# Joining the two halves of the routing sums on VectorE before one turning, instead of turning both and joining after

## The chip, the cores and the metric

The kernel runs on one core of one Trainium2 chip. The metric is device microseconds (us) of one execution; lower is better. Engines: TensorE (PE, with its weight loads shown apart as PEld), VectorE (DVE), ScalarE (ACT), GpSimd (POOL), and SyncE (SP), which issues all DMAs of this kernel.

## The reference, cut to what matters

```python
def reference(x, cond, weights, router_weight, router_bias, expert_bias):
    W = weights[cond]                                    # (64, 128, 128), one of 16 per batch
    h = jnp.einsum('bct,bcd->bdt', x, W)                 # x: (64, 128, 2048) f32
    flat = h.reshape(64 * 128, 2048)
    logits = jnp.einsum('th,eh->te', flat, router_weight) + router_bias    # 64 experts
    scores = jax.nn.softmax(logits, axis=-1)
    topk_w, topk_idx = jax.lax.top_k(scores, 8)
    w_sum = topk_w.sum(axis=-1, keepdims=True)
    w_dense = zeros.at[rows, topk_idx].add(topk_w)       # (8192, 64)
    out = flat * w_sum + w_dense @ expert_bias
    return x + out.reshape(64, 128, 2048)
```

The kernel gets the logits without h: it first forms z = x @ router_weight^T for a batch (128 channels by 64 experts) and then multiplies by the batch's W.

## The kernel before, in words

The 64 batches are taken in 32 pairs. A pair passes through three steps: in its *new* step its x is transposed and multiplied by the router, in its *mid* step the routing is finished (logits, top 8, exponentials, weights), in its *old* step the large product is formed and stored. So one step of the loop works on three pairs at once: new pair i, mid pair i-1, old pair i-2. Each engine has its own program, written out in a fixed order; a step has eight slots, v = 0 to 7, and semaphores tie the engines together. Four steps are unrolled in a loop body.

Products that need more than one pass's precision are made from two parts: a rounded part ("hi") and what is left ("lo"), both in fp32r. The router table router_hl holds hi and lo parts of the 64 experts side by side as 128 columns, so the router product has 128 rows: rows 0 to 63 are the sums with the high part, rows 64 to 127 those with the low part. zt_ps (one PSUM bank) holds that product for both batches of the pair, batch 0 in columns 0 to 127 and batch 1 in columns 128 to 255. High and low rows must still be added, and the sum turned (channels to partitions).

Per step and engine, in the order of the slots:

- TensorE: `transposes` (L325, four 128x128 transposes into a bank of xt_ps; none in slots 2 and 3, where VectorE re-lays the data), `project` (L385, L386, L387, L390, L391: five 512-column matmuls into a bank of p_ps), in slot 0 the last `route` of the mid pair (L337), in slots 2, 4 and 6 a `route` of the new pair (eight 256-column matmuls each), `turn_z` in slot 1 (L351, two transposes of zt_sb into scores_ps, with a wait for zt_ready), `score` in slot 3 (L360), `turn_kept` in slot 7 (L369). In slot 0 of the next step, project's fourth matmul (L390) waits for kept_t_ready.
- ScalarE: `zt_copy` in slot 1 (L470, the whole of zt_ps to zt_sb, 128x256), `xt_high` in each slot (L451), `x_high` (L459), `w_high` in slot 3 (L465), `exponentials` in slot 4 (L478, L482), `norm` in slot 6 (L499, L503), `kept_high` in slot 7 (L490).
- VectorE: `xt_low` in each slot (L546), `finish` in each slot (L612), `relay` at the end of slots 0 and 1 (L556), `z_sum` in slot 2 (L563, adds the two halves of the turned sums into z_sb), `add_bias` in slot 3 (L570), `top` in slot 4 (L577 to L583), `keep` in slot 5 (L591, L595), `kept_low` in slot 7 (L599). Within a slot the order is xt_low, top, kept_low, z_sum, keep, finish, add_bias, relay.
- GpSimd: `x_low` (L681) and `w_low` (L671). SyncE: loads and stores in one fixed order.

A pair's mid step is thus a chain over the engines: last route, zt_copy, turn_z, z_sum, score, add_bias, top, exponentials, keep, norm, turn_kept, kept_high, kept_low, and at its end the L390 of the next step.

Of the kernel before, what the change touches and what calls it, by code (L numbers as in the profile page):

```python
# [36 lines left out]
ALU = mybir.AluOpType  # L37
ACT = mybir.ActivationFunctionType
AX = mybir.AxisListType

P = 128
# [9 lines left out]
def adaln_router(nc, x, condition, weights, router_weight, router_bias, expert_bias, out):  # L51
    B, C, T = x.shape
    S, _, D = weights.shape
    E = router_weight.shape[0]
# [12 lines left out]
    with ExitStack() as ctx:  # L67
        def sb(name, shape, dt=F32):
            return ctx.enter_context(nc.sbuf_tensor(name, shape, dt))

        def bank(name):
            return ctx.enter_context(nc.psum_tensor(name, [P, PIECE], F32))

        def sem(name):
            return ctx.enter_context(nc.semaphore(name))


        ident = sb("ident", [P, P])
# [17 lines left out]
        kept_t_lo = sb("kept_t_lo", [P, 2, 2, P], F32R)  # L96
        w_sum = sb("w_sum", [P, 2, 2])

        zt_sb = sb("zt_sb", [P, 2, P])
        z_sb = sb("z_sb", [P, 2, E])  # L100
        logits = sb("logits", [P, 2, E])
        rest = sb("rest", [P, 2, E])
# [14 lines left out]
        p_ps = [bank(f"p_ps{i}") for i in range(2)]  # L117
        zt_ps = bank("zt_ps")
        scores_ps = bank("scores_ps")
        z_ps = scores_ps[:, 0:4 * E]  # L120
        logits_ps = scores_ps[:, 4 * E:6 * E]
        kept_t_ps = scores_ps[:, 0:2 * P]

# [33 lines left out]
        w_hi_ready = sem("w_hi_ready")  # L157
        w_hl_ready = sem("w_hl_ready")

        zt_ready = sem("zt_ready")  # L160
        z_in_ps = sem("z_in_ps")
        z_ready = sem("z_ready")
        logits_in_ps = sem("logits_in_ps")
# [13 lines left out]
        def is_loop(m):  # L177
            return not isinstance(m, int)

        def wait(eng, s, value):  # L180

            if is_loop(value) or value > 0:
                eng.wait_ge(s, value)
# [17 lines left out]
        def early(m, o):  # L201
            return not is_loop(m) and 4 * m + o < EARLY
# [103 lines left out]
        def _(pe):  # L306
# [21 lines left out]
            def route(m, o, n):  # L328

                i = 4 * m + o  # L330
                if n == 0:
                    wait(pe, zt_ready, i)
                pe.wait_ge(xt_lo_ready, SLOTS * i + 2 * n + 2)
                for q in range(BLOCKS):
                    t = n * BLOCKS + q
                    for xt in (xt_hi, xt_lo):
                        last = pe.matmul(zt_ps[:, 0:2 * P],  # L337
                                         router_hl[:, t, :, :].rearrange("p a e -> p (a e)"),
                                         xt[:, n % 2, q, :, :].rearrange("p r c -> p (r c)"),
                                         start=(t == 0 and xt is xt_hi),  # L340
                                         stop=(t == TB - 1 and xt is xt_lo))
                last.then_inc(routed, 1)

            def turn_z(m, o):

                i = 4 * m + o
                wait(pe, kept_t_ready, i)
                wait(pe, logits_ready, i)
                pe.wait_ge(zt_ready, i + 1)
                for r in range(2):  # L350
                    last = pe.transpose(z_ps[:, r * 2 * E:(r + 1) * 2 * E], zt_sb[:, r, :], ident[:, :])  # L351
                last.then_inc(z_in_ps, 1)

            def score(m, o):

# [8 lines left out]
            def turn_kept(m, o):  # L364

                i = 4 * m + o
                pe.wait_ge(kept_ready, 2 * i + 2)
                for r in range(2):
                    last = pe.transpose(kept_t_ps[:, r * P:(r + 1) * P],  # L369
                                        kept_twice[:, r, :, :].rearrange("p a e -> p (a e)"), ident[:, :])  # L370
                last.then_inc(kept_t_in_ps, 1)
# [24 lines left out]
            for t in range(TB):  # L396
# [8 lines left out]
                last = pe.transpose(p_ps[t // (TB // 2)][:, q * E:(q + 1) * E], block_of_router, ident[0:E, 0:E])  # L405
            last.then_inc(router_in_ps, 1)

            def step(m, j, new, mid, old):
                i = UNROLL + j
                for v in range(SLOTS):  # L410
                    if new and i == 2 and v < 4:
                        if v == 0:
                            for ahead in range(4):
                                transposes(m, i, ahead)
                            turn_kept(m, 0)
                    elif new:
                        transposes(m, i, v)
                    if mid and v == 7 and i != 1:
                        turn_kept(m, i - 1)
                    if old:  # L420
                        if i == 2 and v == 0:
                            pe.wait_ge(expert_ready, 1)
                        project(m, i - 2, v)
                    if mid and v == 3:
                        score(m, i - 1)
                    if mid and v == 1:
                        turn_z(m, i - 1)

                    if mid and v == 0:
                        route(m, i - 1, PIECES - 1)  # L430
                    if new and v in ((2, 4, 6) if old else (3, 5, 7)):
                        if i == 0 and v == 3:
                            pe.wait_ge(router_ready, 2)
                        route(m, i, v // 2 - 1)

            steps(pe, step)


        @block.scalar
        def _(act):  # L440
# [26 lines left out]
            def zt_copy(m, o):  # L467
                i = 4 * m + o
                act.wait_ge(routed, PIECES * (i + 1))
                act.copy(zt_sb[:, :, :], zt_ps[:, 0:2 * P].rearrange("p (r c) -> p r c", r=2)).then_inc(zt_ready, 1)  # L470

            def exponentials(m, o):

# [37 lines left out]
            def step(m, j, new, mid, old):  # L511
                i = UNROLL + j
                for v in range(SLOTS):

                    if new and v == 3:
                        for r in range(2):
                            w_high(m, i, r)
                    if i == 1 and v == 4:
                        act.wait_ge(expert_loaded, 32)
                        act.copy(expert_hl[:, :], expert_sb).then_inc(expert_hi_ready, 1)  # L520
                    if mid and v == 1:
                        zt_copy(m, i - 1)
                    if new:
                        xt_high(m, i, v)
                    if mid and v == 6:
                        norm(m, i - 1)
                    if mid and v == 7:
                        kept_high(m, i - 1)


                    if old and v in (0, 2):
                        x_high(m, i - 2, 1, v // 2)
                    if mid and v in (5, 6):
                        x_high(m, i - 1, 0, v - 5)
                    if mid and v == 4:
                        exponentials(m, i - 1)

            steps(act, step)


        @block.vector
        def _(dve):
# [16 lines left out]

            def z_sum(m, o):  # L560

                dve.wait_ge(z_in_ps, 4 * m + o + 1)
                dve.tensor_reduce(z_sb[:, :, :], z_ps.rearrange("p (r a e) -> p r e a", r=2, a=2),  # L563
                                  AX.X, ALU.add).then_inc(z_ready, 1)

            def add_bias(m, o):
                i = 4 * m + o
# [56 lines left out]
            def step(m, j, new, mid, old):  # L624
                i = UNROLL + j
                for v in range(SLOTS):

                    if mid and v == 4:
                        dve.wait_ge(logits_ready, 4 * m + i)
                    if new:  # L630
                        xt_low(m, i, v)
                    if mid and v == 4:
                        top(m, i - 1)
                    if i == 1 and v == 6:
                        dve.wait_ge(expert_hi_ready, 1)
                        dve.tensor_tensor(expert_hl[E:2 * E, :], expert_sb[E:2 * E, :],
                                          expert_hl[E:2 * E, :].bitcast(F32),
                                          ALU.subtract).then_inc(expert_ready, 1)
                    if mid and v == 7:
                        kept_low(m, i - 1)  # L640
                    if mid and v == 2:
                        z_sum(m, i - 1)
                    if mid and v == 5:
                        keep(m, i - 1)
                    if old:
                        if i == 2 and v == 0:
                            dve.wait_ge(expert_ready, 1)
                        finish(m, i - 2, v)
                    if mid and v == 3:
                        if i == 1:  # L650
                            dve.wait_ge(bias_loaded, 16)
                        add_bias(m, i - 1)
                    if new and (v + 2) // 2 == TURNED and not early(m, i):
                        relay(m, i, v + 2)

            steps(dve, step)


# [59 lines left out]
```

## Time and profile before

| what | value |
|---|---|
| median of 3 runs | 559.85 us (559.28 to 562.32) |
| the profiled execution | 558.69 us, span 556.9 us |
| granted TensorE clock, mean | 0.993 |
| PE busy | 541.0 us, 97% of the span |
| PEld busy | 477.0 us, 86% |
| DVE busy | 471.2 us, 85% |
| ACT busy | 368.5 us, 66% |
| POOL busy | 354.4 us, 64% |
| HBM traffic | 155.96 MB, 280 GB/s over the span |

Busy shares say how full an engine is, not which one sets the end: that is read from which engine never waits. A timeline row gives an instruction's start in us from the span's start, how long it took, its engine and line, what it writes and reads, and in square brackets how long the engine had been idle before it and what ended that. On TensorE, ScalarE and VectorE an instruction may begin before the one ahead of it has ended; the distance from start to start is then what it costs.

### The profile page before, as it was taken

The numbers are of one execution on the slowest core, as the hardware profiler recorded it, in microseconds if no ns is written. First come the engines' busy times: TensorE is split into PE (matmuls) and PEld (weight loads), VectorE is DVE, ScalarE is ACT, GpSimd is POOL, SyncE is SP. The second block draws the span as 40 slices with busy tenths as digits, with TensorE's granted clock in tenths as the row PEclk, the third lists the DMA queues.
The fourth block names the chain that finished last, engine by engine and source line by source line (L and its number), as shares of the span: only waits on it lengthen the run. The fifth ranks groups of instructions, "written<-read, shape, count | busy, mean of one in ns | idle before, by whom it ended". The sixth has DMA issues, their size and how long they took to land.

```text
span 556.9 us, 12892 instructions
## 1 busy us (share of the span) xinstructions
PE 541.0 (97%) x3360; PEld 477.0 (86%) x3360; DVE 471.2 (85%) x1055; ACT 368.5 (66%) x836; POOL 354.4 (64%) x326
## 2 busy tenths in 40 slices
PE   5879999999999999999999999999999999999997
PEld 5768888888888888888888888888888888888875
DVE  2488898988889988889988889898888998888975
ACT  3576666677666677666677666667666667766661
POOL 0176666766666776666776666676666677666676
PEclk9979999999999999999999999999999999999999
DMA  8986999888999888898888999888899888889245
GB/s 243 311 201 231 309 297 279 292 300 287 297 318 276 269 311 289 295 325 280 292 276 296 294 311 300 271 290 297 286 298 315 284 283 295 288 294 326 119 166 212
DMA packets 70850, 155.96 MB, mean 280 GB/s; under 512 B 6322, under 2 KB 45234, under 8 KB 62770
## 3 DMA queue, kind: packets, MB, share of 16 engines
q1 hardware_dynamic: 70834, 155.77, 85.6%
q8 instruction: 7, 0.11, 0.1%
q14 instruction: 9, 0.07, 0.0%
HBM read 88.64 MB, written 67.11 MB: 280 GB/s over the span
## 4 chain that ended last, share of the span: by engine, by line
PE 93%; DMA 3%; SPq 1%; ACT 1%; issue 1%; DVE 1%; ACTq 0%; DVEq 0%
PE zt_ps L337 21%; PE xt_ps L325 14%; PE p_ps L390 11%; PE p_ps L387 11%; PE p_ps L385 11%; PE p_ps L386 10%; PE p_ps L391 10%; PE scores_ps L360 2%; DMA out_sb<-L_ffn_expert_bias 2%; PE scores_ps L369 1%; PE scores_ps L351 1%; DMA cond_sb<-itok_B 1%; SPq L243 0%; SPq L244 0%; DVE xt_lo L546 0%
## 5 line engine op out<-in xcount | busy, mean ns | idle before, releaser
L681 POOL TENSOR_TENSOR x_lo<-x_sb,x_hi 128x512 fp32r<-128x512 f32 x256 | 327.0, 1308 | 176.2 <-ACT x_hi L459 176.2
L546 DVE TENSOR_TENSOR xt_lo<-xt_ps,xt_hi 128x512 fp32r<-128x512 f32 x256 | 175.7, 687 | 63.6 <-ACT xt_hi L451 60.8
L451 ACT CAST xt_hi<-xt_ps 128x512 fp32r<-128x512 f32 x256 | 148.2, 582 | 102.9 <-PE xt_ps L325 84.9
L612 DVE SCALAR_TENSOR_TENSOR out_sb<-p_ps,w_sum,x_sb 128x512 f32<-128x512 f32 x256 | 189.6, 740 | 6.2 <-PE p_ps L391 6.2
L459 ACT CAST x_hi<-x_sb 128x1024 fp32r<-128x1024 f32 x128 | 133.7, 1045 | 0.5 <-PE p_ps L391 0.5
L337 PE MATMUL zt_ps<-xt_hi,router_hl 128*128 128x256 f32 x512 | 129.6, 285 | 4.5 <-DVE xt_lo L546 4.5
L337 PE MATMUL zt_ps<-xt_lo,router_hl 128*128 128x256 f32 x512 | 129.2, 285 | 0.0
L325 PE MATMUL xt_ps<-ident,x_sb 128*128 128x128 f32 x784 | 119.2, 277 | 0.1
L385 PE MATMUL p_ps<-x_hi,w_hl 128*128 128x512 f32 x256 | 118.8, 464 | 0.0
L337 PEld LDWEIGHTS zt_ps<-xt_hi,router_hl 128*128 128x128 f32 x512 | 98.1, 192 | 11.0 <-DVE xt_lo L546 5.2
L337 PEld LDWEIGHTS zt_ps<-xt_lo,router_hl 128*128 128x128 f32 x512 | 98.4, 192 | 4.8
L325 PEld LDWEIGHTS xt_ps<-ident,x_sb 128*128 128x128 f32 x784 | 95.0, 145 | 8.5 <-DMA x_sb<-x 0.5
L390 PE MATMUL p_ps<-expert_hl,kept_t_hi 128*128 128x512 f32 x256 | 101.7, 397 | 0.0
L387 PE MATMUL p_ps<-x_hi,w_hl 128*128 128x512 f32 x256 | 101.2, 395 | 0.0
L386 PE MATMUL p_ps<-x_lo,w_hl 128*128 128x512 f32 x256 | 100.5, 393 | 0.0
L391 PE MATMUL p_ps<-expert_hl,kept_t_lo 128*128 128x512 f32 x256 | 100.2, 391 | 0.0
L556 DVE STREAM_TRANSPOSE xt_ps<-x_turn 128x512 f32<-128x512 f32 x60 | 67.2, 1120 | 0.0
L390 PEld LDWEIGHTS p_ps<-expert_hl,kept_t_hi 128*128 128x128 f32 x256 | 48.1, 188 | 11.6 <-DVE kept_t_lo L599 0.8
L391 PEld LDWEIGHTS p_ps<-expert_hl,kept_t_lo 128*128 128x128 f32 x256 | 48.3, 189 | 11.3
L387 PEld LDWEIGHTS p_ps<-x_hi,w_hl 128*128 128x128 f32 x256 | 48.2, 188 | 10.7
L478 ACT ACTIVATE e_all<-logits,neg_max 128x64 f32<-128x64 f32 x64 | 21.8, 340 | 44.1 <-DVE neg_max L579 44.1
L385 PEld LDWEIGHTS p_ps<-x_hi,w_hl 128*128 128x128 f32 x256 | 48.8, 191 | 1.9 <-issue 1.4
(38 smaller groups left out, 368.7 us busy)
## 6 DMA issues: line engine op xcount, KB each, us to landing
out<-out_sb SPq DMA_DIRECT2D x126, 512.0 KB, 4.2
x_sb<-x SPq DMA_DIRECT2D x62, 1024.0 KB, 6.8
x_turn<-x SPq DMA_DIRECT2D x120, 128.0 KB, 4.7
w_sb<-L_cond_weights SPq DMA_DIRECT2D x64, 64.0 KB, 5.3
x_sb<-x SPq DMA_DIRECT2D x4, 256.0 KB, 6.0
x_sb<-x SPq DMA_DIRECT2D x2, 512.0 KB, 8.0
out_sb<-L_ffn_expert_bias SPq DMA_DIRECT2D x2, 512.0 KB, 9.4
out<-out_sb SPq DMA_DIRECT2D x4, 256.0 KB, 2.5
```

The source lines that it names most:

```text
L325: last = pe.transpose(xt_ps[v % 4][:, q * P:(q + 1) * P], block_of_x, ident[:, :])
L337: last = pe.matmul(zt_ps[:, 0:2 * P], router_hl[:, t, :, :].rearrange("p a e -> p (a e)"), xt[:, n % 2, q, :, :].rearrange("p r c -> p (r ...
L385: pe.matmul(acc, w[:, 0, :], x_hi[:, r, cols], start=True, stop=False)
L386: pe.matmul(acc, w[:, 0, :], x_lo[:, r, cols], start=False, stop=False)
L387: pe.matmul(acc, w[:, 1, :], x_hi[:, r, cols], start=False, stop=False)
L390: pe.matmul(acc, kept_t_hi[:, o % 2, r, :], expert_hl[:, cols], start=False, stop=False)
L391: pe.matmul(acc, kept_t_lo[:, o % 2, r, :], expert_hl[:, cols], start=False, stop=True).then_inc(p_ready, 1)
L451: act.copy(xt_hi[:, n % 2, :, r, :], xt_ps[v % 4][:, :].rearrange("p (q c) -> p q c", c=P)).then_inc(xt_hi_ready, 1)
L459: act.copy(x_hi[:, r, cols], x_sb[:, (2 * o + r) % XRING, cols]).then_inc(x_hi_ready, 1)
L546: dve.tensor_tensor(xt_lo[:, n % 2, :, r, :], xt_ps[v % 4][:, :].rearrange("p (q c) -> p q c", c=P), xt_hi[:, n % 2, :, r, :].bitcast(F32) ...
L612: dve.scalar_tensor_tensor(out_sb[:, r, cols], p_ps[n % 2][:, :], w_sum[:, o % 2, r:r + 1], x_sb[:, (2 * o + r) % XRING, cols], ALU.mult, ...
L681: pool.tensor_tensor(x_lo[:, r, cols], x_sb[:, (2 * o + r) % XRING, cols], x_hi[:, r, cols].bitcast(F32), ALU.subtract).then_inc(x_lo_read ...
```

## The change

`zt_copy` no longer copies all of zt_ps. ScalarE copies two quarters of it, each across the partitions: the low rows of batch 0 (partitions 64 to 127) to partitions 0 to 63 of the new tile z_half, and the high rows of batch 1 (partitions 0 to 63) to partitions 64 to 127. `z_sum` moves from slot 2 to slot 1 and becomes two VectorE additions of 64 rows by 128 columns, PSUM plus z_half, whose results fill the two halves of a zt_sb that is now 128x128: batch 0 on partitions 0 to 63, batch 1 on 64 to 127. `turn_z` moves from slot 1 to slot 2 of TensorE, between project and route, and turns both batches with one transpose. `z_copy` is new: at the head of slot 3 ScalarE copies the turned 128x128 to z_sb.

```diff
-        zt_sb = sb("zt_sb", [P, 2, P])
+        z_half = sb("z_half", [P, P])
+        zt_sb = sb("zt_sb", [P, P])
...
-        z_ps = scores_ps[:, 0:4 * E]
+        z_ps = scores_ps[:, 0:2 * E]
...
             def turn_z(m, o):
                 i = 4 * m + o
                 wait(pe, kept_t_ready, i)
                 wait(pe, logits_ready, i)
-                pe.wait_ge(zt_ready, i + 1)
-                for r in range(2):
-                    last = pe.transpose(z_ps[:, r * 2 * E:(r + 1) * 2 * E], zt_sb[:, r, :], ident[:, :])
-                last.then_inc(z_in_ps, 1)
+                pe.wait_ge(zt_ready, 2 * i + 2)
+                pe.transpose(z_ps, zt_sb[:, :], ident[:, :]).then_inc(z_in_ps, 1)
...
-                    if mid and v == 1:
+                    if mid and v == 2:
                         turn_z(m, i - 1)
...
             def zt_copy(m, o):
                 i = 4 * m + o
                 act.wait_ge(routed, PIECES * (i + 1))
-                act.copy(zt_sb[:, :, :], zt_ps[:, 0:2 * P].rearrange("p (r c) -> p r c", r=2)).then_inc(zt_ready, 1)
+                wait(act, zt_ready, 2 * i)
+                act.copy(z_half[0:E, :], zt_ps[E:2 * E, 0:P]).then_inc(z_half_ready, 1)
+                act.copy(z_half[E:2 * E, :], zt_ps[0:E, P:2 * P]).then_inc(z_half_ready, 1)
+
+            def z_copy(m, o):
+                i = 4 * m + o
+                wait(act, logits_in_ps, i)
+                act.wait_ge(z_in_ps, i + 1)
+                act.copy(z_sb[:, :, :], z_ps.rearrange("p (r e) -> p r e", r=2)).then_inc(z_ready, 1)
...
+                    if mid and v == 3:
+                        z_copy(m, i - 1)
...
             def z_sum(m, o):
-                dve.wait_ge(z_in_ps, 4 * m + o + 1)
-                dve.tensor_reduce(z_sb[:, :, :], z_ps.rearrange("p (r a e) -> p r e a", r=2, a=2),
-                                  AX.X, ALU.add).then_inc(z_ready, 1)
+                i = 4 * m + o
+                dve.wait_ge(z_half_ready, 2 * i + 2)
+                wait(dve, z_in_ps, i)
+                for r in range(2):
+                    rows = slice(r * E, (r + 1) * E)
+                    dve.tensor_tensor(zt_sb[rows, :], zt_ps[rows, r * P:(r + 1) * P], z_half[rows, :],
+                                      ALU.add).then_inc(zt_ready, 1)
...
-                    if mid and v == 2:
+                    if mid and v == 1:
                         z_sum(m, i - 1)
```

The waits of `route` and the semaphore declarations follow the new counts (two increments of zt_ready for each pair).

## Rows read from the trace of the kernel before

**Rows 1.** Busy time of each engine in one long stretch, by windows (x is the count)
```profile
100.00:520.00 420.00, 420.00 (x2642) 372.23 (x2641) 373.07 (x835) 289.87 (x659) 280.87 (x255) 1.00 0.89 292
```

**Rows 2.** ScalarE's timeline, slots 1 to 3 of one step, and the next zt_copy
```profile
302.66 0.37 ACT L470 COPY zt_sb<-zt_ps 128x256 f32<-128x256 f32 x1 [0.50 <-PE zt_ps L337]
303.10 1.16 ACT L451 CAST xt_hi<-xt_ps 128x512 fp32r<-128x512 f32 x2
...
305.10 0.49 ACT L465 CAST w_hl<-w_sb 128x128 fp32r<-128x128 f32 x2
...
319.19 0.37 ACT L470 COPY zt_sb<-zt_ps 128x256 f32<-128x256 f32 x1 [0.50 <-PE zt_ps L337]
```

**Rows 3.** TensorE's timeline of the same step, slots 1 and 2, around turn_z
```profile
303.82 0.40 PE L391 MATMUL p_ps<-expert_hl,kept_t_lo 128*128 128x512 f32 x1
304.05 0.38 PE L351 MATMUL scores_ps<-ident,zt_sb 128*128 128x128 f32 x2
...
304.50 0.39 PE L386 MATMUL p_ps<-x_lo,w_hl 128*128 128x512 f32 x1
...
305.20 0.39 PE L391 MATMUL p_ps<-expert_hl,kept_t_lo 128*128 128x512 f32 x1
```

**Rows 4.** TensorE's timeline late in the run, two projects with nothing between
```profile
535.93 0.39 PE L391 MATMUL p_ps<-expert_hl,kept_t_lo 128*128 128x512 f32 x1
...
536.38 0.39 PE L386 MATMUL p_ps<-x_lo,w_hl 128*128 128x512 f32 x1
```

**Rows 5.** VectorE's timeline of the same step, slots 1 to 4
```profile
303.71 0.69 DVE L546 TENSOR_TENSOR xt_lo<-xt_ps,xt_hi 128x512 fp32r<-128x512 f32 x1
304.32 0.74 DVE L612 SCALAR_TENSOR_TENSOR out_sb<-p_ps,w_sum,x_sb 128x512 f32<-128x512 f32 x1
...
306.59 0.42 DVE L563 TENSOR_REDUCE z_sb<-scores_ps 128x128 f32<-128x256 f32 x1
306.91 0.74 DVE L612 SCALAR_TENSOR_TENSOR out_sb<-p_ps,w_sum,x_sb 128x512 f32<-128x512 f32 x1
...
308.81 0.29 DVE L570 TENSOR_TENSOR logits<-scores_ps,bias_sb 128x128 f32<-128x128 f32 x1
309.27 0.69 DVE L546 TENSOR_TENSOR xt_lo<-xt_ps,xt_hi 128x512 fp32r<-128x512 f32 x1 [0.17 <-ACT xt_hi L451]
```

**Rows 6.** VectorE's timeline near the start, around its one half-row instruction
```profile
32.01 0.69 DVE L546 TENSOR_TENSOR xt_lo<-xt_ps,xt_hi 128x512 fp32r<-128x512 f32 x1 [0.24 <-ACT xt_hi L451]
32.73 2.29 DVE L636 TENSOR_TENSOR expert_hl<-out_sb,expert_hl 64x2048 fp32r<-64x2048 f32 x1
35.05 0.69 DVE L546 TENSOR_TENSOR xt_lo<-xt_ps,xt_hi 128x512 fp32r<-128x512 f32 x1
```

**Rows 7.** VectorE's timeline in the second mid step, add_bias and the next xt_low
```profile
44.59 0.27 DVE L570 TENSOR_TENSOR logits<-scores_ps,bias_sb 128x128 f32<-128x128 f32 x1
44.89 0.69 DVE L546 TENSOR_TENSOR xt_lo<-xt_ps,xt_hi 128x512 fp32r<-128x512 f32 x1
```

**Rows 8.** VectorE's and PEld's timelines, end of the step's chain
```profile
316.70 0.41 DVE L599 TENSOR_TENSOR kept_t_lo<-scores_ps,kept_t_hi 128x256 fp32r<-128x256 f32 x1
...
317.35 0.19 PEld L390 LDWEIGHTS p_ps<-expert_hl,kept_t_hi 128*128 128x128 f32 x1
```

**Rows 9.** The same two, one of the three places where L390 waited
```profile
531.63 0.41 DVE L599 TENSOR_TENSOR kept_t_lo<-scores_ps,kept_t_hi 128x256 fp32r<-128x256 f32 x1
...
532.10 0.19 PEld L390 LDWEIGHTS p_ps<-expert_hl,kept_t_hi 128*128 128x128 f32 x1 [0.30 <-DVE kept_t_lo L599]
532.20 0.19 PEld L391 LDWEIGHTS p_ps<-expert_hl,kept_t_lo 128*128 128x128 f32 x1
```

**Rows 10.** ScalarE's groups by line: busy us, mean ns of one, idle before
```profile
L451 ACT CAST xt_hi<-xt_ps 128x512 fp32r<-128x512 f32 x256 | 148.2, 582 | 102.9 <-PE xt_ps L325 84.9 <-DVE xt_ps L556 16.0
L465 ACT CAST w_hl<-w_sb 128x128 fp32r<-128x128 f32 x64 | 15.8, 295 | 1.7 <-DMA w_sb<-L_cond_weights 1.7
```

**Rows 11.** SyncE's queue in slot 1 and 2 of that step, timeline
```profile
304.40 1.85 SPq L235 DMA_DIRECT2D x_turn<-x  x4
```

More of the change, by code:

```diff
@@ L158, in adaln_router @@
         w_hl_ready = sem("w_hl_ready")
+        z_half_ready = sem("z_half_ready")
         zt_ready = sem("zt_ready")
@@ L331, in route @@
                 if n == 0:
-                    wait(pe, zt_ready, i)
+                    wait(pe, zt_ready, 2 * i)
                 pe.wait_ge(xt_lo_ready, SLOTS * i + 2 * n + 2)
```

## The prediction

> **What bounds the kernel now.** I read the busy shares first, then the windows, then the timelines of single engines over one step. The windows settle the bound: in 420 us in the middle of the run TensorE is busy for all 420.00 us at a granted clock of 1.00 (its full level), VectorE for 373.07 and ScalarE for 289.87 [rows 1]. So in the body TensorE never waits, and the step is as long as its program. ScalarE's zt_copy returns after 319.19 - 302.66 = 16.53 us [rows 2], the length of a step; 32 of them and the two ends make the span. A gain has to take time out of TensorE's own sequence; any other engine's chain counts only where it ends later than TensorE gets there. I call that distance the spare, and look for where the change uses it up.
>
> **TensorE.** With the two transposes of turn_z between two projects, L391 to the next L386 takes 304.50 - 303.82 = 0.68 us [rows 3]; with nothing between, 536.38 - 535.93 = 0.45 [rows 4]. Two transposes cost 0.23 us, one 0.115. The change removes 0.23 from slot 1 and puts one transpose into slot 2, ahead of a route. No row shows a transpose there; it costs between 0 and the 0.23 of the pair, and I take half the pair, since one weight load more stands in the sequence either way. Saved: 0.115 us a step. I count 30 steps (the 25 of the stretch in rows 1 and most of the rest; at both ends TensorE waits for others): 30 x 0.115 = 3.4 us at most, if nothing new is late.
>
> **ScalarE, slot 1.** zt_copy took 0.37 us for 256 columns and starts at 302.66 [rows 2]; the same engine takes 0.582 for 512 columns from PSUM [rows 10], so 0.83 ns a column, and 0.265 for 128. The two w_high take 0.49 together [rows 2] at 0.295 each [rows 10], so neighbours overlap by 0.10. Two half copies then end at 302.66 + 0.265 + 0.165 = 303.09, and the xt_high behind them, which starts at 303.10 [rows 2], is not moved. The bounds are wider, since no row shows a ScalarE instruction that reads one half of the partitions and writes the other: without overlap, with a gap of 0.03, xt_high starts at 303.25 (0.15 late); at 0.295 each, 303.31 (0.21 late); at the full 0.37 each, 303.46 (0.36 late). I take no delay.
>
> **VectorE.** Slot 1 gains two additions between xt_low (303.71) and finish (304.32) [rows 5]. The nearest row is add_bias, 128 columns from PSUM plus SBUF, 0.29 us [rows 5]. VectorE normally starts an instruction about 0.08 before the last has ended (303.71 + 0.69 = 304.40 against 304.32). The one half-row instruction of this kernel, on partitions 64 to 127, breaks that: xt_low ends at 32.70, it starts at 32.73, ends at 35.02, and the next starts at 35.05 [rows 6], 0.03 behind instead of 0.08 ahead, on both sides. Its 2.29 us for 2048 columns also show that half the rows do not halve the time. So the first addition, which starts on partition 0 like its neighbours, runs from 304.32 to 304.61, the second, on partition 64, from 304.64 to 304.93, and finish starts at 304.96: 0.64 later than now. If neither were held it would be 0.42; if the first were held too, 0.75. Slot 2 loses the reduce: 306.91 - 306.59 = 0.32 [rows 5]. Net 0.32 later from there on, bounds 0.10 and 0.43.
>
> The Trainium skill, "VectorE: DVE Perf Modes", section "Two Vector instructions with no wait between them", gives the reason as the start quadrant: an instruction is held until the earlier ones have finished when its operands start in another group of 32 partitions than the last ones used in the same memory. By that rule the second addition and finish are held and the first is not, which gives the same 0.64; rows 6 agree with it (0.03 behind), but show one case only, and read as "a half-row instruction is held" they would hold the first too.
>
> **Is turn_z late?** Its zt_ready comes at 304.93, and a weight load follows its release by 0.06 (531.63 + 0.41 = 532.04 to 532.10 [rows 9]): 304.99. Slot 2's project ends with L391 at 305.20 now [rows 3], 304.97 without the two transposes; the transpose follows at 305.20 and needs its load, which holds the next one up by 0.10 [rows 9], by 305.10. Spare 0.11 us. Behind a late turn_z the route and everything after it would queue on TensorE.
>
> **Is score late?** z_copy (0.27 us by the slope above) waits for a transpose that ends near 305.5 and is done before 305.8; score comes after a route and a project more. Spare over a microsecond. Behind z_copy stand the two w_high and xt_high of slot 3, which now wait for the relay that finish's delay moves by 0.64 anyway, so the wait is hidden under it. finish's new end, 305.70, releases a store whose queue is busy with the x_turn loads until 304.40 + 1.85 = 306.25 [rows 11]: no DMA moves in that slot. finish of slot 3 ends 0.32 later, and holds its store and the next load by as much; that load is for the next step. I cost both at nothing.
>
> **Is the end of the chain late?** This is the tight place. add_bias moves by 0.32. The xt_low behind it could start 0.03 after it (44.86 to 44.89 [rows 7]) but starts 0.17 after, held by xt_high [rows 5], so 0.14 is spare and xt_low, top and the exponentials move by 0.18. From there ScalarE and VectorE hand work to each other without a gap that I could find, so kept_low moves by 0.18 too: its end goes from 317.11 [rows 8] to 317.29, and the load of L390 may start at 317.35. That load starts at 317.35 now [rows 8], with its matmul about 0.23 behind; TensorE comes 0.115 earlier, so the matmul is due at 317.465 and, with 0.10 for the load, the load at 317.365. Spare 0.01 us. What was 0.3 us of spare here is spent, partly because TensorE itself is faster. Every further 0.01 us on VectorE's or ScalarE's chain costs 30 x 0.01 = 0.3 us.
>
> **Sum.** Saved 3.4 us. With a spare of 0.01 and my reading errors near 0.05, which can only cost, I take 0.02 a step back, 0.6 us. Net 2.8: the profiled execution goes from 558.69 (span 556.9 and 1.8 around it) to 555.9. It lies 1.16 below the median of the runs, so on the median's scale 559.85 - 2.8 = 557.0.
>
> **The rivals.**
> - The gain is handed back at L390. If the first addition is held as well, or a semaphore takes 0.1 longer, the chain grows by about 0.1 a step and TensorE waits that long for kept_low: saved 0.115 - 0.10 = 0.015, times 30 = 0.4, time 559.4. For it speaks the spare of 0.01; against it, that each term was read from rows as they stand.
> - ScalarE's copies across the partitions make it slower. If they cost 0.295 and do not overlap, xt_high of slot 1 is 0.21 late, xt_low with it, then both additions and the whole chain; TensorE waits 0.20 at L390 and the step grows by 0.20 - 0.115 = 0.085, times 30 = +2.6, time 562.4; at 0.37 each 0.35 - 0.115, times 30 = +7.0, time 566.9. It decides from a delay of 0.125 on. For it speaks that VectorE's half-row instruction loses its overlap [rows 6]; against it, that ScalarE's time falls with the columns [rows 2, 10].
> - VectorE is not held between halves. Then the chain grows by 0.10, the spare stays at 0.2, and the whole 3.4 stays: 556.4.
> - The transpose ahead of the route costs the full 0.23 and nothing is saved: 559.9 or more. Rows 3 show only a pair, so it cannot be excluded, but I give it little.
>
> **Chances.** Forecast (556.4 to 558.0) 0.45; handed back, with the dear transpose (558.0 to 560.5), 0.30; slower by ScalarE (over 560.5) 0.15; not held (up to 556.4) 0.10. What a measurement of this kernel can tell from no change is about 0.5%, 2.8 us: below 557.05 is faster, over 562.65 slower. Faster gets about two thirds of the forecast case and the last one, 0.40; slower takes the far part of the ScalarE case, 0.12; the rest is the same, 0.48. The range reaches from the whole saving with a margin of 0.4 to the ScalarE case: 556.0 to 562.4.
>
> **What would show it.** In the profile after: one L351 per step, L391 to the second L337 in slot 2 about 0.115 longer than without it; the step at 16.42 to 16.45 us; the two additions 0.29 each, the second and finish 0.03 behind what stands ahead; the two copies near 0.265 with xt_high of slot 1 right behind the transposes of TensorE; a small wait of L390 for kept_low. The forecast is wrong if the idle time of TensorE before L390 or L351 is 0.1 us a step or more, or if the copies push xt_high.

## The result: 1.0% slower, and the profile after

The changed kernel takes 565.38 us (median of 4 runs, 564.91 to 566.39) against 559.57 us before (559.28 to 562.32): ratio 1.0103, 95% interval 1.0085 to 1.0121. The forecast was 557.0, with a range of 556.0 to 562.4; the result lies above it. The profiled execution took 565.57 us, its span 563.7.

First the windows, the stretch of [rows 1], same columns:

```profile
100.00:520.00 420.00, 419.89 (x2591) 363.10 (x2589) 372.45 (x856) 295.89 (x706) 276.15 (x252) 1.00 0.90 290
```

TensorE still reads as busy, 419.89 of 420 us, at the same granted clock. The counts tell more: 2591 matmuls instead of 2642. One transpose less in each of the 25 steps makes about 25 of these 51; the other half is work that was not reached. Matmul ends are modelled, and a matmul whose successor is late simply looks longer. A wait of TensorE shows on its weight loads. Over the same stretch, the waits of PEld (waiter, waited for: us in total, times, longest); the kernel before has no such row there:

```profile
PEld p_ps L390 <- DVE kept_t_lo L613: 7.5, 25, 0.3
PEld scores_ps L352 <- DVE zt_sb L577: 7.0, 25, 0.5
```

TensorE now waits twice in every step: for the two additions (the turn_z of slot 2, now L352) and for kept_low (L390 in slot 0). Part of each is idle time of the loads that was there anyway; what it costs is read from the matmuls. First slot 2, TensorE's timeline:

```profile
308.92 0.39 PE L391 MATMUL p_ps<-expert_hl,kept_t_lo 128*128 128x512 f32 x1
309.14 0.32 PE L352 MATMUL scores_ps<-ident,zt_sb 128*128 128x128 f32 x1
...
309.54 0.28 PE L339 MATMUL zt_ps<-xt_lo,router_hl 128*128 128x256 f32 x1
```

From L391 to the second matmul of the route it takes 0.63 us; in the runs below in which no matmul is late there it takes 0.46. So 0.17 us is lost. Then slot 0, the end of the chain, VectorE and TensorE:

```profile
304.42 0.41 DVE L613 TENSOR_TENSOR kept_t_lo<-scores_ps,kept_t_hi 128x256 fp32r<-128x256 f32 x1
...
304.63 0.40 PE L387 MATMUL p_ps<-x_hi,w_hl 128*128 128x512 f32 x1
304.89 0.50 PE L390 MATMUL p_ps<-expert_hl,kept_t_hi 128*128 128x512 f32 x1
305.23 0.40 PE L391 MATMUL p_ps<-expert_hl,kept_t_lo 128*128 128x512 f32 x1
```

L387 to L391 takes 0.60 us, undisturbed (as in the kernel before) 0.47: 0.13 lost. L390 starts 0.06 behind kept_low's end, as in [rows 9]. The sum, 0.17 + 0.13 - 0.11 saved = 0.19 a step, times 30 = 5.7 us, is near the 5.8 us measured. The step's mean over the stretch went from 16.53 to 16.74 us.

Where the lateness begins is ScalarE's slot 1, against [rows 2]. The last matmul of the route and the transposes of that slot on TensorE, then ScalarE:

```profile
306.28 0.28 PE L339 MATMUL zt_ps<-xt_lo,router_hl 128*128 128x256 f32 x1
306.41 0.60 PE L327 MATMUL xt_ps<-ident,x_sb 128*128 128x128 f32 x4
```

```profile
306.68 0.26 ACT L471 COPY z_half<-zt_ps 64x128 f32<-64x128 f32 x1 [0.71 <-PE zt_ps L339]
306.97 0.26 ACT L472 COPY z_half<-zt_ps 64x128 f32<-64x128 f32 x1
307.25 1.15 ACT L451 CAST xt_hi<-xt_ps 128x512 fp32r<-128x512 f32 x2
```

The route ends at 306.56, the first copy starts 0.11 to 0.12 later (0.04 before the change; in one step of four it is 0.19, at 323.5 for example). The second copy starts behind the end of the first, and xt_high behind the end of the second, with no overlap. The transposes end at 307.01; xt_high starts 0.25 behind them instead of 0.04. VectorE, against [rows 5]:

```profile
307.87 0.69 DVE L556 TENSOR_TENSOR xt_lo<-xt_ps,xt_hi 128x512 fp32r<-128x512 f32 x1
308.48 0.60 DVE L577 TENSOR_TENSOR zt_sb<-zt_ps,z_half 64x128 f32<-64x128 f32 x2
309.11 0.75 DVE L626 SCALAR_TENSOR_TENSOR out_sb<-p_ps,w_sum,x_sb 128x512 f32<-128x512 f32 x1
...
313.30 0.27 DVE L584 TENSOR_TENSOR logits<-scores_ps,bias_sb 128x128 f32<-128x128 f32 x1
313.70 0.69 DVE L556 TENSOR_TENSOR xt_lo<-xt_ps,xt_hi 128x512 fp32r<-128x512 f32 x1
```

From xt_low to finish it is 1.24 us instead of 0.61: the additions delay finish by 0.63, as forecast (0.64). And xt_low of slot 4 starts 0.13 behind add_bias.

### The profile page after: what moved, and what is told of

The parts are those of the page before. It is cut to its first block, busy times and chain, and to the rows that moved or that the text cites. A ratio compares the mean times of both kernels' runs of the same rounds, so it can differ in the third digit from the quotient of the medians.

```text
span 563.7 us, 13038 instructions
## 1 busy us (share of the span) xinstructions
PE 545.2 (97%) x3328; PEld 470.1 (83%) x3328; DVE 476.2 (84%) x1087; ACT 380.9 (68%) x900; POOL 354.1 (63%) x326
## 4 chain that ended last, share of the span: by engine, by line
PE 89%; DMA 3%; DVE 2%; issue 2%; ACT 2%; SPq 1%; ACTq 0%; DVEq 0%
PE zt_ps L339 21%; PE xt_ps L327 14%; PE p_ps L390 11%; PE p_ps L385 10%; PE p_ps L387 10%; PE p_ps L391 10%; PE p_ps L386 10%; DMA out_sb<-L_ffn_expert_bias 2%; PE scores_ps L360 2%; PE scores_ps L369 1%; PE scores_ps L352 1%; DMA cond_sb<-itok_B 1%; ACT xt_hi L451 1%; DVE xt_lo L556 1%; DVE out_sb L626 0%
## 5 line engine op out<-in xcount | busy, mean ns | idle before, releaser
L339 PE MATMUL zt_ps<-xt_hi,router_hl 128*128 128x256 f32 x512 | 131.9, 290 | 5.6 <-DVE xt_lo L556 5.6
L385 PE MATMUL p_ps<-x_hi,w_hl 128*128 128x512 f32 x256 | 116.3, 454 | 0.0
L390 PE MATMUL p_ps<-expert_hl,kept_t_hi 128*128 128x512 f32 x256 | 103.9, 406 | 0.5 <-DVE kept_t_lo L613 0.5
L387 PE MATMUL p_ps<-x_hi,w_hl 128*128 128x512 f32 x256 | 100.9, 394 | 0.0
L391 PE MATMUL p_ps<-expert_hl,kept_t_lo 128*128 128x512 f32 x256 | 100.2, 392 | 0.0
L390 PEld LDWEIGHTS p_ps<-expert_hl,kept_t_hi 128*128 128x128 f32 x256 | 48.0, 187 | 19.5 <-DVE kept_t_lo L613 9.8
L387 PEld LDWEIGHTS p_ps<-x_hi,w_hl 128*128 128x128 f32 x256 | 48.0, 188 | 10.8
L391 PEld LDWEIGHTS p_ps<-expert_hl,kept_t_lo 128*128 128x128 f32 x256 | 48.1, 188 | 9.8
```

Of the source, the lines that this page charges most:

```text
L339: last = pe.matmul(zt_ps[:, 0:2 * P], router_hl[:, t, :, :].rearrange("p a e -> p (a e)"), xt[:, n % 2, q, :, :].rearrange("p r c -> p (r ...
L385: pe.matmul(acc, w[:, 0, :], x_hi[:, r, cols], start=True, stop=False)
L387: pe.matmul(acc, w[:, 1, :], x_hi[:, r, cols], start=False, stop=False)
L390: pe.matmul(acc, kept_t_hi[:, o % 2, r, :], expert_hl[:, cols], start=False, stop=False)
L391: pe.matmul(acc, kept_t_lo[:, o % 2, r, :], expert_hl[:, cols], start=False, stop=True).then_inc(p_ready, 1)
```

## The experiments

Theory A: ScalarE's copies push xt_high of slot 1, with it VectorE's chain, and TensorE waits for that at L352 and L390. Rival B: VectorE's additions alone overrun the chain. Rival C: one transpose ahead of a route is dear in itself. The steps given are means over the stretch of 100 to 520 us, from start to start of the copy of zt_ps.

**xt_high ahead of the copies.**

```diff
-                    if mid and v == 1:
-                        zt_copy(m, i - 1)
                     if new:
                         xt_high(m, i, v)
+                    if mid and v == 1:
+                        zt_copy(m, i - 1)
```

> The changed kernel with one edit: in slot 1 ScalarE does xt_high first and the two half copies behind it. Theory A (the copies push xt_high of slot 1 by 0.25 us behind TensorE's transposes, and everything on VectorE behind it; that is what TensorE waits for at L352 and L390): xt_high starts about 0.03 behind the transposes again, the step falls from 16.71 to 16.42 to 16.46 us, 556 to 558 us, both waits nearly gone. Rival B (VectorE's two additions overrun the chain alone, wherever ScalarE stands): the step stays at 16.6 or more, 562 to 565 us. Rival C (one transpose ahead of a route is dear in itself): L391 to the second matmul of the route stays near 0.63 us although nothing waits.

Measured: 559.08 us, ratio to the kernel before 0.9984 (0.9973 to 0.9995), step 16.49. xt_high is back at 0.04 behind the transposes, and L391 to the second matmul of the route takes 0.46 us. ScalarE's timeline, then TensorE's:

```profile
303.94 0.59 ACT L451 CAST xt_hi<-xt_ps 128x512 fp32r<-128x512 f32 x1 [1.01 <-PE xt_ps L327]
304.55 0.26 ACT L471 COPY z_half<-zt_ps 64x128 f32<-64x128 f32 x1
304.83 0.26 ACT L472 COPY z_half<-zt_ps 64x128 f32<-64x128 f32 x1
```

```profile
305.81 0.39 PE L391 MATMUL p_ps<-expert_hl,kept_t_lo 128*128 128x512 f32 x1
...
306.27 0.28 PE L339 MATMUL zt_ps<-xt_lo,router_hl 128*128 128x256 f32 x1
```

One wait is left, for which A had no reason (PEld's waits, same stretch; L387 to L391 takes 0.54, so 0.075 is lost):

```profile
PEld p_ps L390 <- DVE kept_t_lo L613: 6.4, 26, 0.3
```

So 6.3 of the 9 us between the changed kernel and TensorE's own pace go with ScalarE's order. B as stated and C fall: with the same additions on VectorE the step is 0.25 shorter, and the transpose costs 0.46 - 0.23 - 0.12 = 0.11 (0.23 for a project's last matmul, 0.12 for the route's first). But the step missed the expected 16.46, and 0.075 a step was still to be found.

**Without zt_copy's second wait.**

```diff
                 act.wait_ge(routed, PIECES * (i + 1))
-                wait(act, zt_ready, 2 * i)
                 act.copy(z_half[0:E, :], zt_ps[E:2 * E, 0:P]).then_inc(z_half_ready, 1)
```

> The changed kernel without zt_copy's second wait (on zt_ready, 2 * i), which route's own wait already implies. Theory A: the first copy starts about 0.03 instead of 0.11 us behind the route's last matmul, xt_high 0.08 earlier, the step 16.63, near 563 us. Rivals B and C: no change, 565.4 us.

Measured: 563.56 us, ratio 1.0073 (1.0054 to 1.0091), step 16.63: as A expected. The copy starts 0.04 behind the route (305.53 + 0.28 = 305.81), and the wait at L352 shrinks from 7.0 to 4.4 us:

```profile
305.53 0.28 PE L339 MATMUL zt_ps<-xt_lo,router_hl 128*128 128x256 f32 x1
```

```profile
305.85 0.26 ACT L470 COPY z_half<-zt_ps 64x128 f32<-64x128 f32 x1 [0.62 <-PE zt_ps L339]
306.14 0.26 ACT L471 COPY z_half<-zt_ps 64x128 f32<-64x128 f32 x1
```

```profile
PEld p_ps L390 <- DVE kept_t_lo L612: 7.4, 25, 0.3
PEld scores_ps L352 <- DVE zt_sb L576: 4.4, 25, 0.2
```

A wait that was long met cost 0.08 us. The traces tell what of it costs. They also hold what an engine's sequencer, the part that goes through its waits and counts, does itself (ACTq for ScalarE, DVEq for VectorE). In the loop the count that a wait asks for depends on the loop's number and has to be worked out, by an instruction ALU_OP or FUSED_REGOPS. In the changed kernel the one for the second count stands behind the first wait, between the route's end at 306.56 and the copy at 306.68:

```profile
L185 ACTq ALU_OP  x1: 38/38/38, 306.6 to 306.6; - x1
```

In the steps written out ahead of the loop and behind it the counts are constants. There the changed kernel has both waits three times with no such instruction between, and the copy starts 0.04 behind the route each time, here at 38.80 + 0.28 = 39.08:

```profile
38.80 0.28 PE L339 MATMUL zt_ps<-xt_lo,router_hl 128*128 128x256 f32 x1
...
39.12 0.26 ACT L471 COPY z_half<-zt_ps 64x128 f32<-64x128 f32 x1 [0.79 <-PE zt_ps L339]
```

In all 28 steps of the loop there is one, and the copy starts 0.11 or more behind. By these rows it is not the second wait as such, but the work for its count, done only when the first wait is over. No run put the two waits in the other order, which would test this directly.

**The exponentials' chain earlier, copies as they are.**

```diff
+                    if mid and old and v == 3:
+                        add_bias(m, i - 1)
+                        dve.wait_ge(logits_ready, 4 * m + i)
...
                         finish(m, i - 2, v)
                     if mid and v == 3:
...
-                        add_bias(m, i - 1)
+                        if old:
+                            top(m, i - 1)
+                        else:
...
+                            add_bias(m, i - 1)
```

(In these steps top and its wait are gone from slot 4.)

> The changed kernel with add_bias ahead of finish in slot 3 and top right behind that finish, so that the exponentials' chain gets about 0.35 us back while ScalarE's copies stay as they are. Theory A: L390 no longer waits, but L352 still does, for zt_ready that the copies make late; the step is 16.5 to 16.6 us, 559 to 562 us. Rival B (the chain to kept_low alone): the step falls to 16.42, near 556.5 us. Rival C: 16.5 or more with no wait at L352.

Measured: 562.97 us, ratio 1.0055 (1.004 to 1.0071), step 16.61, a little above A's numbers. L390 no longer waits, L352 does as before:

```profile
PEld scores_ps L352 <- DVE zt_sb L577: 7.1, 25, 0.5
```

So L352's wait does not hang on L390's: with L390's gone it stays at its full 0.17 us (L391 to the route's second matmul takes 0.63). The other way round was not tried.

**Both edits.**

> Both edits together. Theory A: TensorE waits nowhere, the step is TensorE's own program, 16.42 us, 556 to 557 us, about 0.6% below the kernel before. Rival B: the same or a little more. Rival C: the step at 16.53, as before the change, 559.5 us, with L391 to the route's second matmul near 0.6 us.

Measured: 556.12 us, ratio 0.994 (0.9921 to 0.9959), step 16.42. Neither L352 nor L390 is among PEld's waits in the stretch; the one row is

```profile
PEld xt_ps L327 <- issue: 0.5, 1, 0.5
```

This beats both kernels, and is near the 556.4 that the prediction gave for the whole of the saving.

**What was left in the first experiment.** Add_bias ahead of finish, top where it was:

```diff
+                    if mid and v == 3:
...
+                        add_bias(m, i - 1)
                     if old:
...
                         finish(m, i - 2, v)
-                    if mid and v == 3:
...
-                        add_bias(m, i - 1)
```

> The kernel of the first experiment (xt_high ahead of the copies) with one more edit: add_bias ahead of finish in slot 3, top left where it is, so that the wait for logits_ready ahead of xt_low in slot 4 is met before VectorE gets there. Theory D (in the loop that xt_low starts 0.13 us behind add_bias because VectorE waits for its own result, and this is the spare that the prediction counted twice): the gap of 0.13 goes, L390 stops waiting (it lost 0.075 a step), the step falls from 16.49 to 16.42, near 556.5 us. Rival E (VectorE is simply full from kept_low to there, the order does not matter): the step stays at 16.49, 559 us.

Measured: 556.38 us, ratio 0.9953 (0.9935 to 0.9971), step 16.41, no wait of PEld in the stretch. VectorE in slots 3 and 4, first in the first experiment, then here:

```profile
309.97 0.28 DVE L584 TENSOR_TENSOR logits<-scores_ps,bias_sb 128x128 f32<-128x128 f32 x1
310.37 0.69 DVE L556 TENSOR_TENSOR xt_lo<-xt_ps,xt_hi 128x512 fp32r<-128x512 f32 x1
```

```profile
307.52 0.27 DVE L584 TENSOR_TENSOR logits<-scores_ps,bias_sb 128x128 f32<-128x128 f32 x1
307.71 0.73 DVE L626 SCALAR_TENSOR_TENSOR out_sb<-p_ps,w_sum,x_sb 128x512 f32<-128x512 f32 x1
308.37 0.67 DVE L556 TENSOR_TENSOR xt_lo<-xt_ps,xt_hi 128x512 fp32r<-128x512 f32 x1
```

Before, xt_low started 0.12 behind the end of add_bias (ScalarE's xt_high had ended at 309.96, long before); now everything overlaps by 0.07 to 0.08. Theory D holds, E falls: the same instructions in another order gave the 0.08 a step back.

Why the wait for the own result takes 0.13, the traces tell as they did for the copy. In the changed kernel an ALU_OP for the next wait's count stands between the end of add_bias (313.57) and xt_low (313.70):

```profile
L555 DVEq ALU_OP  x1: 45/45/45, 313.6 to 313.6; - x1
```

The loop of the third experiment has both cases for finish, which there waits for add_bias:

```profile
278.04 0.27 DVE L584 TENSOR_TENSOR logits<-scores_ps,bias_sb 128x128 f32<-128x128 f32 x1
278.44 0.75 DVE L626 SCALAR_TENSOR_TENSOR out_sb<-p_ps,w_sum,x_sb 128x512 f32<-128x512 f32 x1
```

```profile
311.21 0.27 DVE L584 TENSOR_TENSOR logits<-scores_ps,bias_sb 128x128 f32<-128x128 f32 x1
311.52 0.75 DVE L626 SCALAR_TENSOR_TENSOR out_sb<-p_ps,w_sum,x_sb 128x512 f32<-128x512 f32 x1
```

In 14 steps such an ALU_OP stands between the two, and finish starts 0.13 behind the end of add_bias, as at 278.44; in the other 14 none does, and it is 0.04, as at 311.52.

**Control: that reordering in the kernel before.** Slot 3 of VectorE as in the fourth experiment, nothing else.

> The kernel before with only the reordering of VectorE in slot 3 that the fourth experiment had (add_bias ahead of finish, top behind it). A control. Theory A (before the change TensorE's own program is the step): the step stays at 16.533, no change, 559.5 us. Rival F (the reordering by itself is what made the fourth experiment fast): 556 to 557 us.

Measured: 560.06 us, ratio 1.0009 (0.9996 to 1.0022), step 16.533. No change: the reordering alone brings nothing, and the 0.6% of the fourth experiment is the transpose taken away.

**ScalarE's copy in two halves, nothing crossing, in the kernel before.**

```diff
-                act.copy(zt_sb[:, :, :], zt_ps[:, 0:2 * P].rearrange("p (r c) -> p r c", r=2)).then_inc(zt_ready, 1)
+                for rows in (slice(0, E), slice(E, 2 * E)):
+                    last = act.copy(zt_sb[rows, :, :], zt_ps[rows, 0:2 * P].rearrange("p (r c) -> p r c", r=2))
+                last.then_inc(zt_ready, 1)
```

> The kernel before with zt_copy in two instructions, partitions 0 to 63 and 64 to 127, 256 columns each, nothing crossing the partitions. Theory G (a ScalarE instruction that starts on another partition than the last one waits for its end): the second copy starts 0.02 to 0.03 us behind the first one's end and xt_high as much behind the second's, 0.40 us behind TensorE's transposes instead of 0.04; the old chain's spare (0.31 at L390 and 0.04 ahead of slot 4's xt_low) takes it nearly whole, so the step is 16.53 to 16.56, 559.5 to 561 us. Rival H (only crossing partitions costs the overlap): the second copy starts 0.10 ahead of the first one's end, xt_high 0.2 late, the step 16.533, 559.5 us.

Measured: 561.69 us, ratio 1.0051 (1.0032 to 1.007), step 16.57, a little more than expected.

```profile
304.07 0.75 ACT L471 COPY zt_sb<-zt_ps 64x256 f32<-64x256 f32 x2 [0.49 <-PE zt_ps L337]
304.84 1.07 ACT L451 CAST xt_hi<-xt_ps 128x512 fp32r<-128x512 f32 x2
```

The two copies of 0.37 take 0.75 together, and xt_high starts 0.02 behind them: no overlap, with rows that stay on their partitions. H falls, and the starts are those that theory G gave. But wherever a 64-row instruction of ScalarE stands close to another one in these runs, the start partition changes too, so G and the plainer rival that 64 rows by themselves cost the overlap are not told apart. Part of the cost came at another place than I expected:

```profile
PEld scores_ps L360 <- issue: 4.8, 25, 0.2
PEld p_ps L390 <- DVE kept_t_lo L601: 0.3, 2, 0.2
```

```profile
308.36 0.40 DVE L565 TENSOR_REDUCE z_sb<-scores_ps 128x128 f32<-128x256 f32 x1
```

```profile
308.88 0.52 PEld L360 LDWEIGHTS scores_ps<-z_sb,w_sb 128*128 128x128 f32 x4 [0.19 <-issue]
```

The profile names no releaser for L360, but its load starts 0.12 us behind the end of z_sum, which it needs. L391 to the transposes behind score takes 0.64 us instead of 0.62: 0.02 of the 0.035 that the step grew by. So the kernel before had a third place with little spare, score's wait for z_sum in slot 3. That it is z_sum is read from the times, not tried.

## Why the prediction was wrong, step by step

- **The bound was right.** TensorE's own program is the step, and one transpose less takes 0.11 to 0.12 us from it: forecast 0.115, measured 16.53 to 16.41 or 16.42 wherever no matmul is late (fourth and fifth experiments). The transpose ahead of a route costs half of the pair, so the rival of the dear transpose falls.
- **VectorE's additions were right**: 0.63 for 0.64, the second held, finish held, the first not. The Trainium skill's rule on start quadrants ("VectorE: DVE Perf Modes", section "Two Vector instructions with no wait between them") agrees with it: within the pair, 0.60 = 0.27 + 0.03 + 0.29, and finish 0.03 behind.
- **The step that failed is "ScalarE, slot 1 ... I take no delay".** xt_high was 0.21 us late. Most of it, 0.13, is the overlap (what stays in the second experiment, 0.17 behind the transposes instead of 0.04): I took it from w_high, a pair of whole tiles [rows 2], for instructions that change their start partition, though VectorE's [rows 6] had just shown that such a change can break it; the bound of 0.15 stood beside it and was nearly the right value. The Trainium skill, "ScalarE: Activation LUTs", section "What ACT_TABLE_LOAD costs", says that back-to-back ACTIVATEs overlap by about 93 ns; [rows 2, 10] agree for whole tiles (0.10), and the halves of the after and of the last experiment do not: the measurement decides. The rest, 0.08, is a term that I did not have at all: the wait that the change adds ahead of the copy, with its count worked out behind the first wait (second experiment). The kernel before showed its size: where such an instruction (here FUSED_REGOPS) stands behind the release, xt_high starts 0.11 behind the end of the transposes (here 299.91 + 0.60 = 300.51) and not 0.04.

```profile
299.91 0.60 PE L325 MATMUL xt_ps<-ident,x_sb 128*128 128x128 f32 x4
```

```profile
300.62 0.59 ACT L451 CAST xt_hi<-xt_ps 128x512 fp32r<-128x512 f32 x1 [0.83 <-PE xt_ps L325]
```

- **The spare at the end of the chain was 0.10 too large.** "0.14 is spare" ahead of slot 4's xt_low rested on [rows 7], one of the steps written out ahead of the loop, where xt_low starts 0.03 behind add_bias. In the loop it is 0.12 to 0.13 (after, first experiment). In [rows 5] the gap of 0.17 was put down to ScalarE's xt_high, which did come last there; the own wait of VectorE lay hidden only 0.04 under it. So the 0.01 that I called spare was a deficit of about 0.09, and the first experiment shows it alone: 0.075 a step. The 0.13 has an ALU_OP in it, which the steps written out do not have (fifth experiment).
- **The size, then.** The ScalarE rival gave 562.4 for a delay of 0.21. Add the 0.10 of the spare that was not there, times 30 = 3.0, and it is 565.4, which was measured. The chain is then 0.30 later than an undelayed TensorE could take it; TensorE loses 0.17 of that at L352 and the other 0.13 at L390. That it comes out to 0.1 us is luck, since each term is read to 0.01 us, 0.3 us over 30 steps. That the rival's 0.21 was right is luck too: it stood there for copies of 0.295 without overlap, and came from copies of 0.26 without overlap and the 0.08 that no rival had.
- **turn_z's spare** was 0.04 and not 0.11. Of a lateness of 0.21 TensorE lost 0.17 at L352, and of 0.13 in the second experiment it lost 0.09. The moment of release was forecast well; the moment by which the load must start was put about 0.08 too late. In the first experiment (and so in the fourth and fifth), with the additions ending at 305.17 + 0.60 = 305.77, the load of L352 just meets its turn, 0.23 behind the load ahead of it, and nothing is lost:

```profile
305.59 0.19 PEld L391 LDWEIGHTS p_ps<-expert_hl,kept_t_lo 128*128 128x128 f32 x1
305.82 0.14 PEld L352 LDWEIGHTS scores_ps<-ident,zt_sb 128*128 128x128 f32 x1
```


What stays open: why the load ahead of a transpose must start earlier than the one of L390, and whether ScalarE loses its overlap by the start partition or by the 64 rows.

## What to carry to other kernels

A saving on the engine that sets the end uses up the spare of every chain that engine waits for, and what the change adds to those chains uses it from the other side: add both before calling a place safe, at each place where the engine waits. Durations of half-partition instructions are easy to forecast, their overlap is not: take none where they start on another partition than their neighbours, and put such instructions behind the one that the chain needs. An added wait has a price in a loop, where its count is worked out behind another wait. A spare read between two waits of one instruction is only the distance to the second-latest of them, and must be read in the same kind of step, in the loop and not ahead of it.

## What the runs showed of the hardware that I had not expected

- ScalarE started each 64-row instruction that begins on another partition than the last one, and the full one behind it, only behind the end of the last: gaps of 0.01 to 0.03 us instead of an overlap of 0.10, with crossing rows and without. On VectorE the 64-row addition that starts on the same partition as its neighbour kept its overlap of 0.08; no ScalarE row shows that case.
- The work for a wait's count (ALU_OP, FUSED_REGOPS), when it stands behind another wait of the same instruction, delays the start: on ScalarE 0.11 us behind the releasing matmul instead of 0.04, on VectorE 0.13 behind its own last result instead of 0.03 to 0.04.
- Half the partitions do not shorten a ScalarE copy: 0.37 us for 64x256, as for 128x256; half the columns do, 0.26 for 64x128 and 0.27 for 128x128.
